# Fold stage of a cross-attention and butterfly-FFN kernel: how the butterfly coefficients are loaded and spread, and in which order

## The reference, cut to what matters

```python
def butterfly(y, weights, dim):                 # weights: (11 stages, dim/2, 2, 2)
    for stage in range(weights.shape[0]):
        s = 2 ** stage; nb = dim // (2 * s)
        yr = y.reshape(*lead, nb, 2, s)
        a, b = yr[..., 0, :], yr[..., 1, :]
        w = weights[stage].reshape(nb, s, 2, 2)
        y = jnp.stack([w[...,0,0]*a + w[...,0,1]*b, w[...,1,0]*a + w[...,1,1]*b], axis=-2).reshape(*lead, dim)
    return y

x = x + layernorm(x) * scan(r = 0.9 * r + ctx * ctx, along the sequence)      # x, ctx: 32 x 512 x 512
h = layernorm(x) @ W_exp + b_exp                 # 512 -> 2048
h = gelu(butterfly(h, up_weights) + up_bias)     # exact gelu
h = butterfly(h, down_weights)
x = x + h @ W_con + b_con + down_bias            # 2048 -> 512
```

## Time and profile before

| | us |
|---|---|
| median of 3 runs | 2802.72 |
| lowest, highest | 2802.57, 2806.71 |
| the profiled execution | 2804.95 |
| its span | 2803.1 |

### The profile page before, as it was taken

How to read it: one execution, slowest core, us unless ns; L and a number is a source line. 1 busy time by engine, 2 the same in 40 slices (tenths; PEclk the granted TensorE clock), 3 DMA queues, 4 the chain that set the end, 5 groups by cost and what they waited for, 6 DMA issues and landing times.

```text
span 2803.1 us, 35216 instructions
## 1 busy us (share of the span) xinstructions
PE 2749.5 (98%) x12281; PEld 2272.2 (81%) x12281; DVE 2126.2 (76%) x3558; ACT 1149.5 (41%) x1700; POOL 396.2 (14%) x568
## 2 busy tenths in 40 slices
PE   8879999999999999999999999999999999999999
PEld 6748888888888888888888888888888888888887
DVE  7768777887877788787778878777887877788533
ACT  6753433434343343434334343433434343343432
POOL 4621111010111101011110201111020111102000
PEclk8889999999999999999999999999999999999999
DMA  8696575856757585665758567575857657585543
GB/s 212 174 336 191 170 211 155 250 164 201 204 167 214 154 251 164 203 204 166 216 158 242 165 203 203 166 221 157 239 165 209 197 167 224 153 243 163 181 150 99
DMA packets 293924, 540.44 MB, mean 193 GB/s; under 512 B 38718, under 2 KB 102366, under 8 KB 276854
## 3 DMA queue, kind: packets, MB, share of 16 engines
q1 hardware_dynamic: 287382, 534.80, 64.5%
q0 software_dynamic: 1520, 2.27, 0.4%
q10 hardware_dynamic: 4848, 1.13, 0.2%
HBM read 447.89 MB, written 56.62 MB: 180 GB/s over the span
## 4 chain that ended last, share of the span: by engine, by line
PE 94%; DMA 3%; DVE 1%; SPq 1%; ACT 1%; issue 0%; DVEq 0%; ACTq 0%
PE ps L1482 43%; PE ps L1500 25%; PE ps L1513 25%; DMA wcon<-in_L_ffn_W_con_dram 1%; DMA kv<-in_ctx_dram 1%; PE ps L1343 0%; PE ps L1391 0%; PE ps L1382 0%; SPq L450 0%; DMA w_products<-xop 0%; DVE w1r L1002 0%; DMA w_split<-w2s 0%; ACT Z L741 0%; PE ps L1562 0%; PE ps L1399 0%
## 5 line engine op out<-in xcount | busy, mean ns | idle before, releaser
L1482 PE MATMUL ps<-xop,w1r 128*128 128x512 f32 x5376 | 1365.7, 390 | 7.1 <-ACT st L858 4.8
L1482 PEld LDWEIGHTS ps<-xop,w1r 128*128 128x128 f32 x5376 | 1010.4, 188 | 218.9 <-DVE xop L1088 5.2
L1500 PE MATMUL ps<-w2r,ghi 128*128 128x512 f32 x2048 | 630.5, 389 | 0.0
L1513 PE MATMUL ps<-w2r,ghi 128*128 128x512 f32 x2032 | 626.1, 389 | 3.7 <-DVE x L1184 3.7
L858 ACT ACTIVATE st<-ps 128x512 f32<-128x512 f32 x384 | 229.7, 598 | 838.6 <-PE ps L1482 838.4
L1184 DVE TENSOR_TENSOR x<-ps,x 128x512 f32<-128x512 f32 x508 | 348.9, 687 | 280.4 <-PE ps L1513 277.8
L1513 PEld LDWEIGHTS ps<-w2r,ghi 128*128 128x128 f32 x2032 | 381.6, 188 | 83.3 <-DVE x L1184 4.1
L1500 PEld LDWEIGHTS ps<-w2r,ghi 128*128 128x128 f32 x2048 | 384.4, 188 | 79.8
L862 ACT ACTIVATE g<-g,gelu_bias 128x512 f32<-128x512 f32 x384 | 275.2, 717 | 368.7 <-DVE g L1202 368.7
L1202 DVE TENSOR_TENSOR g<-ps,st 128x512 f32<-128x512 f32 x384 | 262.8, 684 | 215.5 <-PE ps L1482 215.2
L1207 DVE TENSOR_TENSOR glo<-g,ghi 128x512 fp32r<-128x512 f32 x510 | 345.5, 698 | 79.6 <-ACT ghi L876 79.5
(11 more groups left out here) (138 smaller groups left out, 1651.3 us busy)
## 6 DMA issues: line engine op xcount, KB each, us to landing
w1r<-w_products SPq DMA_DIRECT2D x889, 256.0 KB, 3.3
w2r<-w_split SPq DMA_DIRECT2D x128, 1024.0 KB, 5.0
x<-in_x_dram SPq DMA_DIRECT2D x128, 256.0 KB, 7.0
raw<-kv SPq DMA_DIRECT2D x496, 64.0 KB, 2.3
out_dram<-x SPq DMA_DIRECT2D x120, 256.0 KB, 4.1
kv<-in_ctx_dram SPq DMA_DIRECT2D x64, 256.0 KB, 7.4
raw<-in_ctx_dram SPq DMA_DIRECT2D x64, 256.0 KB, 5.1
w_split<-w2s SPq DMA_DIRECT2D x12, 512.0 KB, 6.7
```

Source lines behind the costliest of these rows:

```text
L1482: last = nc.tensor.matmul(bank[:, :], w1r[:, slot, w, c * P:(c + 1) * P], xop[:, XPOS[m], v, c, :], start=(opens and i == 0), stop=(i == l ...
L1500: last = nc.tensor.matmul(ps_ya[j][:, :], g[:, p % 2, q, j * P:(j + 1) * P], w2r[:, p % 2, kk, w, :], start=(p == 0 and kk == 0 and i == 0 ...
L1513: last = nc.tensor.matmul(ps_yb[:, :], g[:, p % 2, q, j * P:(j + 1) * P], w2r[:, p % 2, kk, w, :], start=(kk == 0 and i == 0), stop=(kk == ...
```

## The change

- **Loads.** `load_coefs` loads stages 0 and 1 (`WHOLE`) with one DMA of 16 partitions by whole rows; stages 2 to 5 as before. `load_top` loads 4 rows of 4 KB and broadcasts nothing. Up's loads go on ACT's queue, ahead of everything on ACT; SP's order is `wexp` 0 to 3, high up, kv, x half 0, x half 1, `wcon` 0; after low_up top down and ctx half 1; after the low down spread `wcon` 1.
- **Spreads.** Stages 0 and 1: DVE lays the coefficients out in three copies (`lane_rows`) and PE spreads them by 6 matmuls against the identity (`whole_spread`). Stages 4 and 5: high parts at lane 0 and low parts at lane Q = 32 of one tile, so that one matmul with the selector stacked twice (`sel_parts`) does both (`parted_spread`; 6 matmuls where there were 12). Top stage: the same with `top_sel`, 8 matmuls into four banks (`top`), and DVE multiplies straight from PSUM, four operations (`top_products`). `pick` and `pick_second` go.
- **Zeroing.** The lanes between are set to zero: on DVE for up, ahead of WT 1; on POOL for down.
- **PE's order.** The top spread up stands before WT 12, the spread of high up before low_up, the top spread down after `high_up`.
- **FOLD.** ACT keeps WT 4 to 10 alone; DVE keeps WT 1, 3, 11, 13, 15.
- **ACT's order.** `square(0, 0)` moves to before the third low_up step, the down `coefs_hi` to before the sixth and ninth; `top_hi` follows `coefs_hi(0)` and low_up.
- **DVE's order**, as in the diff. **POOL**: selectors in another order, `high_matrix(0)` ahead of `rstd_rows(0)`, and the wait for `low_matrix_ready` 2 moves from `first_moves(0)` to `weight_sums(0)`; SP's wait for it goes.

```diff
+        def top_part(dn, lane):
+            return top_parts[dn][lane:lane + 4].rearrange("q (b x) -> q b x", b=2)
+        TOP_PLACE = [(0, 1, 2, 3), (0, 1, 2, 4)]
...
         def load_coefs(eng, weights, dn):
-            for stage in range(LOWS):
+            eng.dma_start(low_rows[dn], weights[0:len(WHOLE)].rearrange("s (k n) a b -> k s (n a b)", k=KH))\
+               .then_inc(low_loaded[dn], NX)
+            for stage in range(len(WHOLE), LOWS):
...
         def load_top(eng, weights, dn):
-            eng.dma_start(top_src[dn], weights[LOW - 1].rearrange("m a b -> (m a b)").partition_broadcast(P))\
-              .then_inc(top_loaded[dn], NX)
+            eng.dma_start(top_src[dn][0:4], weights[LOW - 1].rearrange("(o n) a b -> o (n a b)", o=4))\
+               .then_inc(top_loaded[dn], NX)
...
+            def lane_rows(dn):
+                dve.wait_ge(low_loaded[dn], LOW_LOADS * NX)
+                if dn:
+                    dve.wait_ge(coef_spread, len(WHOLE))
+                for stage in WHOLE:
+                    n = 1 << stage
+                    src = low_rows[dn][:, stage, :].rearrange("k (q n b) -> k n q b", n=2 * n, b=2)
+                    to = low_lanes[:, 2 * n - 2:4 * n - 2, :].rearrange("k n (q b m) -> k n q b m", b=2, m=n)
+                    for m in range(n):
+                        nc.vector.tensor_copy(to[:, :, :, :, m], src).then_inc(lanes_ready, 1)
...
+            def top_products(dn):
+                dve.wait_ge(path_product, spreads(dn, LOWS - 1))
+                dve.wait_ge(top_spread, dn + 1)
+                for c, bank in enumerate(TOP_PLACE[dn]):
+                    last = path_stage(nc.vector, flat(LX[:, dn, 4 * c:4 * c + 4, :]), half[:, 2 * c * P:2 * (c + 1) * P],
+                                      spread_view(ps[bank][:, :], 0, LOW - 1, KH // 4), LOW - 1)
+                last.then_inc(low_matrix_ready, 1)
...
             for k in range(KH // 4):
                 fold_step("WT", k)
+            dve.wait_ge(sel_ready, 2 * len(PARTED))
+            for lane in (0, Q):
+                nc.vector.tensor_copy(sel_parts[lane:lane + Q], sel[0:Q, PARTED[0]:LOWS]).then_inc(sel_rounded, 1)
+            dve.wait_ge(top_sel_ready, 2)
+            for lane in (0, Q):
+                nc.vector.tensor_copy(top_sel[lane:lane + Q], top_choice[0:Q]).then_inc(top_sel_ready, 1)
+            lane_rows(0)
             coefs_lo(0)
+            top_lo(0)
             low_products(0)
-            dve.wait_ge(path_product, LOWS)
-            dve.wait_ge(top_picked, 2)
-            top_stage(nc.vector, 0).then_inc(low_matrix_ready, 1)
+            top_products(0)
             for k in range(KH // 4, KH):
                 fold_step("WT", k)
-            coefs_lo(1)
...
-            for j in range(J):
-                scan_chunk(0, 0, j)
+            scan_chunk(0, 0, 0)
+            scan_chunk(0, 0, 1)
+            lane_rows(1)
+            coefs_lo(1)
+            scan_chunk(0, 0, 2)
+            scan_chunk(0, 0, 3)
+            high_products(0)
             stats1(0, 0, xs[0], range(J))
...
-            high_products(0)
             for j in range(J):
                 normalise(0, 0, xs[0], j)
+            top_lo(1)
             low_products(1)
-            dve.wait_ge(path_product, spreads(1, LOW - 2))
-            dve.wait_ge(top_picked, 4)
-            top_stage(nc.vector, 1).then_inc(low_matrix_ready, 1)
...
             gate(1, 1, xs[0], 0)
+            top_products(1)
             weights_lo(0)
...
+                def top():
+                    pe.wait_ge(top_sel_ready, 4)
+                    pe.wait_ge(coef_lo, dn * PARTS + PARTS)
+                    pe.wait_ge(path_product, ALL_DONE if dn else LOWS)
+                    for c, bank in enumerate(TOP_PLACE[dn]):
+                        for bit in range(2):
+                            last = nc.tensor.matmul(ps[bank][:, :], top_sel[0:Q + 4, c, bit, :],
+                                                    top_parts[dn][0:Q + 4, bit * 512:(bit + 1) * 512],
+                                                    start=(bit == 0), stop=(bit == 1))
+                    last.then_inc(top_spread, 1)
...
             for k in range(KH):
+                if k == 2:
+                    square(0, 0)
+                if k in (5, 8):
+                    coefs_hi(1, k // 8)
                 fold_step("low_up", k)
...
             rstd_rows(1)
             wait_kept(pool, "high_up", R - 1)
+            pool.wait_ge(low_matrix_ready, 2)
             weight_sums(0)
```

More of the change, by code:

```diff
@@ L267, in supers @@
                 body(u, u % 2, first=False, last=(u == U - 1))
-        FOLD = [("WT", k, "dve" if k % 2 and not KH // 4 < k < KH // 2 - 1 else "act") for k in range(KH)]
+        FOLD = [("WT", k, "dve" if k % 2 and not KH // 4 <= k < KH // 2 + 2 else "act") for k in range(KH)]
         FOLD += [("low_up", k, "act") for k in range(KH)]
@@ L298, in xattn_ffn_program, with low_part, low_whole, parts_zero @@
         LOWS = LOW - 1
+        WHOLE = range(2)
         PARTED = range(LOWS - 2, LOWS)
+        PARTS = len(PARTED) + 1
+        def low_part(dn, stage, lane):
+            rows, off, n = src_place(stage)
+            return low_parts[dn][lane:lane + rows, off:off + n].rearrange("q (b x) -> q b x", b=2)
+        def low_whole(dn, stage):
+            rows, off, n = src_place(stage)
+            return low_src[dn][0:rows, off:off + n].rearrange("q (x b) -> q b x", b=2)
+        def parts_zero(dn):
+            first, last = src_place(PARTED[0])[1], sum(src_place(PARTED[-1])[1:])
+            return low_parts[dn][0:Q, first:last].bitcast(f32)
         def spreads(dn, stage):
@@ L600, in _, with choose @@
             pool.wait_ge(sel_zero, 1)
-            for stage in range(LOWS):
+            def choose(stage):
                 rows = (P // 2) >> stage
@@ L933, in _, with spread_view, path_products @@
                 .then_inc(mask_ready, 1)
-            def path_products(dn, first, stages, places, full, spare, outer, before_last=None):
+            def spread_view(a, first, stage, outer):
+                order = "p (o a l) -> p o a l"
+                if not first and stage in WHOLE:
+                    order = "p (l a o) -> p o a l"
+                if not first and stage >= PARTED[0]:
+                    order = "p (o l a) -> p o a l"
+                return a.rearrange(order, o=outer, a=2, l=1 << stage)
+            def path_products(dn, first, stages, places, full, spare, outer):
                 prev = None
                 for stage in range(stages):
-                    if before_last and stage == stages - 1:
-                        before_last()
                     n = outer << (stage + 1)
@@ L945, in path_products @@
                     if prev is None:
-                        last = nc.vector.tensor_copy(cur, ps[bank][:, col:col + n])
+                        last = nc.vector.tensor_copy(cur.rearrange("p (o a l) -> p o a l", o=outer, a=2),
+                                                     spread_view(ps[bank][:, col:col + n], first, stage, outer))
                     else:
@@ L1369, in high @@
                     for b in range(HIGH):
-                        stage_spread((high_src[dn],), sel[:, b], HIGH_PLACE[b], b, "q (l o a b) -> q o a l b")
-                return low, high
+                        stage_spread(high_src[dn], HIGH_PLACE[b], b, "q (l o a b) -> q o a l b")
+                return low, high, top
             def fold_step(kind, i):
```

198 lines of the change are left out of this document (108 added, 90 removed).

## The result

| | before | after |
|---|---|---|
| median, us | 2804.83 | 2819.55 |
| lowest, highest | 2802.57, 2806.71 | 2817.47, 2822.56 |
| runs | 6 | 6 |
| profiled execution, its span | 2804.95, 2803.1 | 2819.41, 2817.6 |

The ratio is 1.0053, with a 95% interval of 1.004 to 1.0066: the changed kernel is slower by 14.7 us, 11 to 19 by the interval. Between the profiled executions it is 2819.41 - 2804.95 = 14.5. The forecast was 2814.2, a shift of 11.5, with a range of 2799 to 2821. The time lies in the range, but above the 2809 to 2818 that the forecast gave for its own case. Of the 5.35 us between 2814.2 and 2819.55, 2.1 are the median of the kernel before, which was 2802.72 when the shift was added to it and is 2804.83 here; 3.2 are the shift itself.

A forecast was written before the change was run, and what follows sets the result against it. The prediction took DVE's row of work in the fold, started by ACT's square of ctx, as the bound, not the wcon load. It summed 12.6 - 1.1 = 11.5 us onto 2802.7, giving 2814.2, range 2799 to 2821.

The forecast's parts named there:

- its own case: Main forecast: DVE's row of work ends the fold later; 2814.2 us, from 2809 to 2818, chance 0.53.
- DVE's parts done: Start of the fold: DVE's casts, lane copies, low parts and the top's low parts done at 20.4 us.
- narrow spreads, wide spreads done: PE before the first low matrix: 20 small instructions for stages 0 to 3 end at 19.8, six wide matmuls at 22.8.
- half-1 scan: Start of DVE's first scan of half 1, forecast at 86.3 us, where it was 77.25.
- POOL's sums: Start of POOL's first weight sum, after the wait for low_matrix_ready 2, forecast at 112.6 us.
- first high_dn copy: ACT's first kept high_dn step, after POOL's sums and ACT's rounding, forecast at 117.5 us instead of 104.94.
- The 1.1 us given back: At high_dn: PE runs on without the cold start behind its wcon wait, regaining about 1 us within eight steps.
- the 0.4 put down for waits: Between gate 0 of half 1 and POOL's sums: 0.4 us added for waits beside top_products(1).
- The port: DVE statistics beside POOL's high_matrix(0): claimed not held through the shared port; held in full, 2.9 us more, 2817.1.
- Clock stays up: Rival at the spreads before low_up: PE keeps 2.4 GHz, so the shift is 5.0 us, 2807.7; chance 0.22.
- wcon and PE are the bound: Rival for the fold: the wcon load and PE bound it, not DVE; 9.7 us faster, 2793.0; chance 0.12.
- Slower still: Rival: statistics held by POOL (2.9), top spread at half clock (2.0), dearer casts (1); 2820, chance 0.13.

The follow-up runs named there:

- g2_all: Changed kernel; ACT keeps WT 11, square and down high parts earlier, top_products(1) before gate 0, POOL's low_up wait later: 0.8 us above before, ratio 1.0001.
- e6_wt11_act: Changed kernel, but ACT instead of DVE keeps transpose step WT 11: 9.2 us above the kernel before, ratio 1.0034.
- e5_wcon_late: Changed kernel, but the first half of wcon is loaded behind the second, after the low down spread: 13.5 us above the kernel before, ratio 1.005.
- e2_square_hi_first: Changed kernel, but ACT's square and the down high parts stand before its first low_up step: 8.0 us above the kernel before, ratio 1.0029.
- g1_pool_order: e2_square_hi_first, with POOL's wait for low_up and its memset behind high_matrix(0) and rstd_rows(0): 4.5 us above the kernel before, ratio 1.0016.
- h1_split: g2_all, but ACT's third rounding of the first weight group goes behind the first four high_dn copies: 0.8 us above the kernel before, ratio 1.0002.
- f1_scans_early: Changed kernel reordered: kv behind wexp, early square, two scans before top products, WT 11 on ACT, down parts and top products earlier: 5.6 us above before, 1.0022.

## Why the prediction was right, and where it was short

| step | worked out | measured after |
|---|---|---|
| DVE's parts done | 20.4 | 19.5 |
| narrow spreads, wide spreads done | 19.8, 22.8 | 19.0, 21.8 |
| top spread done | 30.4 | 29.7 |
| top products done, low matrix | 33.0 | 32.3 |
| PE done with WT 15 | 34.6 | 34.8 |
| high spread done | 38.5 | 39.6 |
| ACT's first low_up copy | 39.4 | 41.60 |
| DVE's first scan | 43.15 | 46.18 |
| scans done | 59.9 | 62.8 |
| half-1 scan | 86.3 | 89.22 |
| gate of half 1 | 106.9 | 109.82 |
| POOL's sums | 112.6 | 114.82 |
| first high_dn copy | 117.5 | 119.20 |
| time - before | 11.5 | 14.7 |

**The mechanism was right.** DVE's own row of work is what ends the fold, ACT's square in low_up starts it, and everything later moves with it. The edits that move the square, the parts and the top products gave back what they had been charged, and the whole shift is gone in g2_all. The low matrix came at 32.3 for the reasons given: WT 4 to 11 and the top spread stand ahead, and the preparation of parts takes DVE longer. That this first stretch agrees to 0.9 us is in part luck. PE's first transposes came 1.1 us earlier than before (6.29 against 7.35) where the forecast had them 0.7 later, DVE's casts began at 10.27 and not at 12.3, and its copies then waited until 12.93 for the coefficients, a wait that the forecast didn't have. (Its terms, 0.8 + 1.5 + 1.0 + 1.21 + 2.28 + 1.2, are 8.0 and not 8.2.)

**The mis-sized term** is the stretch from WT 15 to the first scan, 8.5 us worked out (34.6 to 43.15) and 11.4 measured (34.8 to 46.18). The text did see PE wait for WT 11's bank ("Only then does it keep WT 11, 13 and 15, for whose banks PE waits"), but kept the high spread at 3.90 and the first low_up steps at 0.90, their durations at the full clock. They were 4.84, and 2.1 and 1.7 a step. That is 0.9 + 1.2 + 0.8 = 2.9, the whole miss at the first scan. By e6_wt11_act the 0.9 come from the wait, and the 2.0 from the place of the high spread: they are there without the wait too, and the kernel before has them behind the same spread (its steps of 1.70 us at high_up, above), where the forecast could have read them. The wait itself is worth 2.2 + 0.9 (transposes) + 0.95 (high spread) = 4.05 of the 4.66 that this kernel won; the rest was there before it (the top spread began 0.5 earlier in that execution, and these 0.5 can't be put down to the edit).

**The 1.1 us given back** by "PE then runs on without the cold start" didn't come. PE no longer waits 4.82 for wcon but 5.23 for ACT at 120.39, and starts cold there as well. The shift is 14.3 at the first high_dn copy, 15.1 at PE's last high_dn step (136.67 against 121.55), and 14.6 at the last wait of the first products (194.07 against 179.47).

**Between scan and sums** small errors cancel in part. From the half-1 scan to the gate it took 20.60, as worked out. From the gate to the sums it took 5.0 instead of 5.7, because gate 0 took 2.4 beside an idle POOL and not 2.7, and the 0.4 put down for waits were 0.1. From the sums to the first copy 4.4 instead of 4.9. The 3 us at the scans are 1.7 at the first copy; with the 1.1 that weren't given back this is 2.8 of the 3.2 by which the time was missed, and the rest is below what the runs can tell.

**The port.** The statistics beside `high_matrix(0)` took 2.46 (64.00 to 66.46, POOL's operation from 64.22), and 2.43 where POOL was idle: not held. The rule of the Trainium skill ("SBUF — State Buffer", "Who interferes with whom") was the right one for this term, and the 2817.1 that holding would have given is ruled out as a mechanism. An operation with two tensor inputs (`carry` and `kvT`, L1082) that began beside POOL's was held in this kernel as in the one before: 3.14 us from 97.27, while POOL worked from 96.69 to 100.36, where its neighbour took 0.19.

**The rivals.** *Clock stays up* (2807.7): refuted; the granted clock was 0.50 from 14 to 26, and the first part of the chain ran as worked out with the half clock. (the earlier trace rows are of the wide spreads, though, not of the narrow ones, which ran from 10.93 to 15.24: there the clock was 1.00 and then 0.75.) *wcon and PE are the bound* (2793.0): refuted by e5_wcon_late. *Slower still* (2820): its time is the nearest to the measured one, but its mechanism didn't happen: the statistics weren't held, the top spread took 2.11, at the full clock, and the four casts took 2.3, as worked out. The 3.2 us that the forecast was short came from elsewhere, as told above; that 2820 is so near is chance.

**What the forecast missed altogether** is POOL's new wait for the end of low_up, with `high_matrix(0)` and `rstd_rows(0)` behind it. It costs nothing in the kernel after, and 4 us as soon as the scans are early (e2_square_hi_first against g1_pool_order).

## What to carry to other kernels

Follow the engine whose row of work reaches to the end of the stage rather than the wait that is longest: sending the load that the chain named so late that PE stood 8.88 us for it cost nothing that could be measured, while repairs on ACT, DVE and POOL took back the whole 14.7. When a step is moved in one engine's queue, list what is queued behind every wait, on all engines; the square, 10 us early, brought 1.2 until the parts were moved too, the parts brought 4 less than they could until POOL's memset was moved, and one repair (h1_split) only made the next wait. And look at the clock behind a PE stall and behind narrow matmuls before you take over a duration: here a stall of 2.2 us cost 1.9 more at half clock, while in the kernel before one of 2.46 us cost nothing more.

## What the runs showed of the hardware

- Small loads that were issued first, on ACT's queue from 0.75 us on, were there at 12.9 us only, with 4 MB of `wexp` issued beside them on SP's queue from 0.74 on; with 3 MB of these held back they were there by 9.98. PE's first transposes, which wait for the first 1 MB of `wexp`, began at 6.29 in the kernel after, at 7.07 in h1_split and at 6.66 with the rest held back.
- Behind a 2.22 us wait of PE the granted clock was 0.50 for 8 us (34 to 42), through transposes, narrow spread and low_up, though PE was busy throughout. Without the wait it was 1.00 from 24 to 34, then 0.71, 0.50 and 0.94 in three stretches of 2 us around and behind the end of the narrow spread (34.90). In the kernel before it stayed at 1.00 behind a wait of 2.46 us (36.47), and was 0.61 and 0.53 from 76 to 80, behind a narrow spread and no wait.
- The eight top spreads of 512 columns took 2.11 us (0.26 each) at the full clock, the six wide ones 2.92 (0.49 each) at the half clock, in the same kernel. In f1_scans_early the eight top spreads ran at 0.50 and took 3.78 (0.47 each).
- A DVE statistics operation with one input wasn't held by POOL's `tensor_tensor` beside it (2.46 against 2.43 for four); one of two inputs and 16 columns was, for 3.14 us instead of 0.19.
